# Eight pairs' statistics moved from VectorE to ScalarE, new idle products on TensorE, and new orders for all five engines

## The reference

```
layer 0 and 1 (graph attention):
    h = x W^T;  e_ij = leaky(h_i.a_src + h_j.a_dst, 0.2), -inf where adj == 0
    layer(x) = softmax_j(e) h
layer 2:
    e_ij = leaky(sum_d x_id a0_d x_jd, 0.2)     # adj == 1 takes e0; 2, 3, 4 don't occur in a 0/1 matrix
    layer(x) = (sigmoid(e) where adj == 1, else 0) x + bias2
layer 3:
    layer(x) = ((adj == 1) x) W3[0] + bias3
layernorm: (x - mean) / sqrt(var + 1e-5), over the 128 features
```

## Time and profile before

| | us |
|---|---|
| three runs, median (lowest, highest) | 241.93 (241.18, 242.17) |
| the profiled execution's own time | 242.28 |
| its span, from first to last instruction | 240.2 |
| busy: TensorE, its weight loads, VectorE | 221.1, 205.2, 217.6 |
| busy: ScalarE, GpSimd | 190.6, 171.6 |
| mean granted TensorE clock | 0.979 of full speed |

### The profile page before, as it was taken

The page is one execution under the profiler, slowest core; times in us unless marked ns, Lnnn a source line. Parts: engine busy times, 40 slices in busy tenths (PEclk is TensorE's granted clock), DMA queues, the critical chain, the costliest instruction groups (busy, mean ns, idle before and its releaser), DMA issues.

```text
span 240.2 us, 5686 instructions
## 1 busy us (share of the span) xinstructions
PE 221.1 (92%) x1737; PEld 205.2 (85%) x1737; DVE 217.6 (91%) x716; ACT 190.6 (79%) x613; POOL 171.6 (71%) x262
## 2 busy tenths in 40 slices
PE   7598998999999999999999999999999999799760
PEld 7497977898979999999989999999999899799650
DVE  1568997999999998999999999999999999999992
ACT  2466799696989788857877998698866999999872
POOL 5120541399889878866497988694989989999991
PEclk9979999999999999999999999999999999999995
DMA  7996910332322100801400580004000021000115
GB/s 178 257 199 152 239 50 5 129 50 42 44 90 46 66 26 0 264 1 44 134 1 4 87 262 3 1 4 132 3 0 0 3 89 48 0 0 3 45 42 183
DMA packets 12144, 17.56 MB, mean 73 GB/s; under 512 B 1104, under 2 KB 5968, under 8 KB 12112
## 3 DMA queue, kind: packets, MB, share of 16 engines
q1 hardware_dynamic: 9520, 12.85, 16.4%
q0 software_dynamic: 2304, 4.20, 10.7%
q10 hardware_dynamic: 288, 0.14, 0.2%
HBM read 17.17 MB, written 4.19 MB: 89 GB/s over the span
## 4 chain that ended last, share of the span: by engine, by line
PE 73%; DVE 14%; ACT 5%; issue 3%; DMA 3%; POOL 1%; DVEq 0%; POOLq 0%
PE banks L1189 32%; PE banks L1124 10%; PE banks L1156 10%; PE banks L1146 5%; PE banks L1109 4%; PE banks L1186 4%; PE banks L1166 4%; DVE fstats L918 3%; DMA mask_all<-adj_turned 3%; DVE wgt_all L865 3%; DVE fres_all L910 3%; DVE fres_all L898 2%; ACT odd_square L610 1%; PE banks L1134 1%; ACT wgt_all L665 1%
## 5 line engine op out<-in xcount | busy, mean ns | idle before, releaser
L547 POOL TENSOR_TENSOR frstd<-fvar,minus_half 128x4 f32<-128x4 f32 x64 | 65.1, 1023 | 15.6 <-DVE fvar L924 6.2
L1189 PE MATMUL banks<-vals_all,wgt_all 128*128 128x129 f32 x512 | 63.6, 279 | 0.0
L1189 PEld LDWEIGHTS banks<-vals_all,wgt_all 128*128 128x128 f32 x512 | 61.0, 194 | 1.0
L865 DVE SCALAR_TENSOR_TENSOR wgt_all<-banks,gain,mask_all 128x256 f32<-128x256 f32 x128 | 52.5, 470 | 0.8 <-DMA mask_all<-adj_turned 0.4
L918 DVE BATCH_NORM_STATS2 fstats<-fres_all 128x6 f32<-128x256 f32 x128 | 46.9, 414 | 0.1
L542 POOL TENSOR_TENSOR xb_all<-xs_all,bias_cen 128x256 f32<-128x256 f32 x64 | 45.3, 732 | 1.0 <-ACT xs_all L692 0.9
L692 ACT ACTIVATE xs_all<-fres_all,frstd 128x128 f32<-128x128 f32 x112 | 35.9, 404 | 1.4 <-POOL frstd L547 1.3
L1189 PE MATMUL banks<-xs_all,wgt_all 128*128 128x128 f32 x256 | 31.3, 276 | 1.5 <-DVE wgt_all L873 1.4
L1189 PEld LDWEIGHTS banks<-xs_all,wgt_all 128*128 128x128 f32 x256 | 29.9, 192 | 2.0 <-DVE wgt_all L873 1.9
L1156 PE MATMUL banks<-fxT,fxTa 128*128 128x256 f32 x128 | 30.3, 382 | 0.0
L1156 PEld LDWEIGHTS banks<-fxT,fxTa 128*128 128x128 f32 x128 | 23.1, 190 | 2.8 <-issue 0.2
(11 more groups left out here) (92 smaller groups left out, 400.7 us busy)
## 6 DMA issues: line engine op xcount, KB each, us to landing
xT_all<-x_turned SPq DMA_DIRECT2D x16, 256.0 KB, 3.2
mask_all<-adj_turned POOLq DMA_DIRECT2D x16, 256.0 KB, 4.7
x_all<-x_laid SPq DMA_DIRECT2D x16, 256.0 KB, 4.0
out<-xs_all SPq DMA_DIRECT2D x16, 256.0 KB, 2.3
bias<-biases_laid SPq DMA_DIRECT2D x1, 128.0 KB, 6.1
w_pack<-W_and_columns ACTq DMA_DIRECT2D x1, 68.0 KB, 3.1
w_fast<-W_turned ACTq DMA_DIRECT2D x1, 64.0 KB, 3.4
w_nat<-in_L_gnn_W SPq DMA_DIRECT2D x1, 64.0 KB, 6.2
```

Source lines behind the costliest of these rows:

```text
L547: nc.gpsimd.tensor_tensor(frstd[:, int(l), slot(n), :], fvar[:, int(l), slot(n), :], minus_half[:, :, :], ALU.pow).then_inc(fast_pool[k], 1)
L865: last = nc.vector.scalar_tensor_tensor(out=wgt(u)[:, c, :], in0=place(f"rows{l}", u), scalar=gain[:, u, c, 1:2], in1=maskT(u)[:, c, :], o ...
L1189: last = nc.tensor.matmul(place(f"out{l}", u)[:, b * width:(b + 1) * width], wgt(u)[:, c, b * P:(b + 1) * P], (vals if l in "01" else xs)( ...
```

## The change

1. ScalarE gets a step `stats` (function `statistics`). Eight pairs' statistics go there from VectorE: `stats2:6`, `stats2:9`, `stats3:1`, `3:3`, `3:4`, `3:6`, `3:7`, `3:8`. For each graph it runs two ACTIVATEs with the function Square over a 128x128 block, which write their squares into `xs` (overwritten later by the norm) and add up a row into `fstats` column 2. The two functions `variances` that looked for `stats` on VectorE now ask `doer`.
2. Idle products: a word `idle:87` puts 8 products into bank 7, without a wait; `idle:97` 9 into bank 7. `warm:3` and `warm:4` are gone, and `warm:5` is there in place of the latter.
3. The last pair's (`SHARED = 15`) final norm is split: VectorE normalizes its first graph and SyncE stores it; ScalarE's new step `last:15` normalizes the second graph and issues its store from its own queue.
4. All five lists and `BANKS` are written anew. Most steps move by a few places. These change engine: `logits0:5` from VectorE to ScalarE; `norm2:1` from VectorE to ScalarE; `norm1:0`, `1:3`, `1:7`, `1:12` from ScalarE to GpSimd and `norm1:5` back; `xTa:7`, `xTa:9` from ScalarE to GpSimd and `xTa:1` back; `bias2:3` and five `fscale` from GpSimd to VectorE, one `fscale` the other way; and some `var`.

Of the tables the diff shows two lines of ScalarE's and two of TensorE's.

```diff
--- before.py
+++ after.py
@@ -55,6 +55,7 @@
 H = 2
 TEAMS = 16
 AHEAD = 6
+SHARED = 15
 X_IN, XT_IN, MASK, XS, FXT, FXTA, VALS, WGT, SG, FRES, XB = 4, 3, 16, 6, 7, 5, 6, 7, 2, 9, 5
 
 
@@ -62,116 +63,115 @@
 ORDER = {
...
     "pe": (
-        "h0:1 h0:0 rows0:1 dT0:1 turn:0 top0:1 dT0:0 warm:3 rows0:0 top0:0 out0:1 warm:4 h0:3 h0:2 dT0:3 h0:4 top0:3 "
+        "h0:1 h0:0 dT0:1 rows0:1 dT0:0 idle:87 turn:0 top0:1 idle:97 top0:0 rows0:0 out0:1 warm:5 h0:3 h0:2 dT0:3 h0:4 "
...
     "act": (
-        "logits0:1 gains0:1 logits0:0 seen:1 v0:1 gains0:0 vals0:1 v0:0 seen:2 seen:3 vals0:0 logits0:2 logits0:3 "
+        "logits0:1 gains0:1 seen:1 logits0:0 v0:1 gains0:0 vals0:1 seen:3 v0:0 seen:2 vals0:0 logits0:2 logits0:3 "
...
-WHOLE = tuple(n + l for n in ("dT", "top", "gains", "v", "logits", "peak", "dmax", "rsum", "rinv", "var", "center", "pow") for l in "0123") + ("fscale", "seen", "res2", "res3")
+WHOLE = tuple(n + l for n in ("dT", "top", "gains", "v", "logits", "peak", "dmax", "rsum", "rinv", "var", "center", "pow") for l in "0123") + ("fscale", "last", "seen", "res2", "res3")
@@ -203,7 +203,7 @@
         if name in apart:
             continue
         for u in graphs(n):
-            if u == n * H or name + layer not in WHOLE:
+            if u == n * H or name + layer not in WHOLE and (name + layer, n) != ("norm3", SHARED):
                 value[n % K] += 1
             found[name + layer, u] = value[n % K]
     return found, value
@@ -212,7 +212,7 @@
 UP_SQUARE = UP * UP
 
 
-COUNTS = {"pe": counts("pe", apart=("turn", "warm")), "act": counts("act"), "dve": counts("dve", apart=("centre", "judge")), "pool": counts("pool", apart=("mask",))}
+COUNTS = {"pe": counts("pe", apart=("turn", "warm", "idle")), "act": counts("act"), "dve": counts("dve", apart=("centre", "judge")), "pool": counts("pool", apart=("mask",))}
 
 
 def at(engine, name, u):
@@ -483,6 +483,9 @@
             def store(l, n, k):
                 normer = doer("norm3", n)
                 sp.wait_ge(signals[normer][k], at(normer, "norm3", final(n)))
+                if n == SHARED:
+                    sp.dma_start(out[n * H], xs(n * H)[:, :, :]).then_inc(fast_stored[n % XS], 16)
+                    return
                 sp.dma_start(out[n * H:(n + 1) * H].rearrange("h p b d -> p h b d"), xs_all[:, pair(n, XS), :, :]).then_inc(fast_stored[n % XS], 16)
 
             def load_weights(l, n, k):
@@ -495,7 +498,7 @@
             sp.wait_ge(redo_set, 1)
             again = sp.value_load(redo_i[0:1, 0:1], min_val=0, max_val=1)
             for q in range(XS):
-                sp.wait_ge(fast_stored[q], 16 * len(range(q, TEAMS, XS)))
+                sp.wait_ge(fast_stored[q], 16 * (len(range(q, TEAMS, XS)) + (q == SHARED % XS)))
             with sp.If(again):
                 sp.dma_start(w3[:, 1:R, :], W3[1:R].rearrange("r d o -> d r o")).then_inc(gen_w3_in, 16)
                 for k, vector in enumerate((bias2, bias3)):
@@ -571,7 +574,8 @@
                     nc.gpsimd.tensor_scalar(fxTa(u)[:, :], fxT(u)[:, :], a2[:, 0:1], None, ALU.mult).then_inc(fast_pool[k], 1)
 
             def variances(l, n, k):
-                pool.wait_ge(fast_dve[k], at("dve", f"stats{l}", final(n)))
+                squarer = doer(f"stats{l}", n)
+                pool.wait_ge(signals[squarer][k], at(squarer, f"stats{l}", final(n)))
                 squares, var = fstats[:, slot(n), :, 2], fvar[:, int(l), slot(n), :]
                 factor, floor = VARIANCE[l]
                 nc.gpsimd.tensor_scalar(var, squares, factor, floor, ALU.mult, ALU.add).then_inc(fast_pool[k], 1)
@@ -692,13 +696,31 @@
                             last = nc.scalar.activation(xs(u)[:, b, :], fres(u)[:, b, :], ACT.Copy, scale=frstd[:, int(l), u, b:b + 1])
                     last.then_inc(fast_act[k], 1)
 
+            def statistics(l, n, k):
+                adder = doer(f"res{l}", n)
+                for u in graphs(n):
+                    act.wait_ge(signals[adder][k], at(adder, f"res{l}", u))
+                    for b in range(NB):
+                        last = nc.scalar.activation(xs(u)[:, b, :], fres(u)[:, b, :], ACT.Square, accum_out=fstats[:, u, b, 2:3])
+                    last.then_inc(fast_act[k], 1)
+
             def variances(l, n, k):
-                act.wait_ge(fast_dve[k], at("dve", f"stats{l}", final(n)))
+                squarer = doer(f"stats{l}", n)
+                act.wait_ge(signals[squarer][k], at(squarer, f"stats{l}", final(n)))
                 factor, floor = VARIANCE[l]
                 nc.scalar.activation(fvar[:, int(l), slot(n), :], fstats[:, slot(n), :, 2], ACT.Copy, bias=floor, scale=factor).then_inc(fast_act[k], 1)
 
-            steps = {"seen": note_odd, "var": variances, "xT": copy_xT, "logits": logits, "gains": gains, "v": exponentials, "vals": values, "xTa": copy_xTa, "sigmoid": sigmoids,
-                     "high": high_part, "agg": copy_gathered, "norm": normalize}
+            def last_norm(l, n, k):
+                u = final(n)
+                act.wait_ge(fast_pool[k], at("pool", "pow3", n * H))
+                for b in range(NB):
+                    normed = nc.scalar.activation(xs(u)[:, b, :], fres(u)[:, b, :], ACT.Copy, scale=frstd[:, 3, u, b:b + 1])
+                normed.then_inc(fast_act[k], 1)
+                act.wait_ge(fast_act[k], at("act", "last", n * H))
+                act.dma_start(out[u], xs(u)[:, :, :]).then_inc(fast_stored[n % XS], 16)
+
+            steps = {"stats": statistics, "seen": note_odd, "var": variances, "xT": copy_xT, "logits": logits, "gains": gains, "v": exponentials, "vals": values, "xTa": copy_xTa, "sigmoid": sigmoids,
+                     "high": high_part, "agg": copy_gathered, "norm": normalize, "last": last_norm}
             for step, l, n in order("act"):
                 steps[step](l, n, n % K)
 
@@ -812,7 +834,7 @@
                         dve.wait_ge(fast_stored[n % XS], 16 * (n // XS))
                 else:
                     dve.wait_ge(fast_pool[k], at("pool", f"pow{l}", n * H))
-                for u in graphs(n):
+                for u in graphs(n)[:1 if (l, n) == ("3", SHARED) else H]:
                     for b in range(NB):
                         if l == "1":
                             last = nc.vector.tensor_scalar(xs(u)[:, b, :], fres(u)[:, b, :], frstd[:, 1, u, b:b + 1], fcenter[:, u, b:b + 1], ALU.mult, ALU.add)
@@ -918,7 +940,8 @@
                     nc.vector.bn_stats(fstats[:, u, :, :].rearrange("p b k -> p (b k)"), fres(u)[:, :, :].rearrange("p b d -> p d b")).then_inc(fast_dve[k], 1)
 
             def variances(l, n, k):
-                dve.wait_ge(fast_dve[k], at("dve", f"stats{l}", final(n)))
+                squarer = doer(f"stats{l}", n)
+                dve.wait_ge(signals[squarer][k], at(squarer, f"stats{l}", final(n)))
                 squares, var = fstats[:, slot(n), :, 2], fvar[:, int(l), slot(n), :]
                 if l == "1":
                     nc.vector.scalar_tensor_tensor(out=var, in0=squares, scalar=1 / D, in1=fvar[:, 0, slot(n), :],
@@ -1207,7 +1230,9 @@
             pe.wait_ge(ident_bf_set, 2)
             sequence = order("pe")
             for q, (step, l, n) in enumerate(sequence):
-                if step == "warm":
+                if step == "idle":
+                    idle_products(n // 10, n % 10)
+                elif step == "warm":
                     following, layer, m = sequence[q + 1]
                     keep_warm(n, following + layer, m * H)
                 else:
```

## The result

The changed kernel takes 246.10 us (median of 4 runs, 244.69 to 247.26), the kernel before 241.79 us in the same comparison (241.18 to 242.17). The ratio is 1.018, with a 95% interval from 1.015 to 1.022: 4.3 us slower. The prediction was 244.4 us, slower, with a range of 240.4 to 246.4. The direction holds, and so does the first half of the term called deciding, a TensorE held by the mask. The fall of the clock behind it, its other half, did not come, and two of the smaller terms have the wrong sign. That the total still lies in the range is in part luck.

The account below looks back on a forecast made before the run. TensorE's pace was taken to bound the middle, its handoffs with VectorE the start and end. 242.28 + 3.4 - 0.5 - 0.2 - 0.2 = 244.8 us, less 0.35 for the profiled execution: 244.4 us, range 240.4 to 246.4.

Parts of the forecast that it names:

- the term called deciding: Start of the lists: TensorE held about 3 us by the mask, then a clock fall; 3.4 us late.
- The fall of the clock: Start, behind the wait: clock at half speed for 4 us, adding 2.0 us; likelier 2 to 1.
- the prediction's case of a wait without the fall: Start: h0:2 ends at 20.4 us, 1.7 us late, clock staying up; kernel 242.7 us, chance 0.22.
- The rival in which the idle products work as they read: Start: logits0:0 before 8 us, no TensorE gap, clock at 1.00; kernel 239.3 us, chance 0.13.
- The middle (-0.5 us): From 60 to 200 us: VectorE's relief meets a full TensorE and wins only 0.5 us.
- net about 5 us off: VectorE's busy time: 5.9 us of statistics and norm2:1 leave, bias2:3, fscale and var come; net about 5 us less.
- The Trainium skill's rule that it weighed: Middle: judge TensorE by the weight loads' busy share; several microseconds could be won; the prediction's counting decided against it.
- ScalarE (10 to 16 us, taken 13): ScalarE's added busy time for 32 squares, 0.32 to 0.51 us each depending on whether the read hides.
- the 124 named as a sign: From 60 to 200 us: ScalarE busy for 124 us or more, beside a full TensorE.
- The rival in which ScalarE is late: Middle: vals and xT copies wait behind squares, TensorE waits 2.4 us more; kernel 246.8 us, chance 0.08.
- The end (-0.4 us): End: 0.2 us won by the shared last norm and store, 0.2 us by earlier res3:10 and out3:12.

Follow-up runs that it names:

- Kernel four: The kernel before with the changed start alone (mask wait ahead of logits0:0 and dT0:0, plus the new idle products); 244.96 us, ratio 1.012.
- kernel five: The changed kernel with the last pair whole again: last:15 removed, one norm on VectorE, one store; 246.14 us, ratio 1.018.
- Kernel seven: The changed kernel with the eight pairs' statistics back on VectorE, all other orders as changed; 248.19 us, ratio 1.028.
- kernel one: The changed kernel with one swap on ScalarE: logits0:0 ahead of seen:1 again; 245.16 us, ratio 1.014.
- kernel three: The kernel before with the new idle products alone, nothing newly waiting for the mask; 242.60 us, ratio 1.003.
- kernel ten: The kernel before with the eight pairs' statistics as squares on ScalarE, and var2:9 on GpSimd; 253.40 us, ratio 1.049.
- kernels five and six: Five has its own line. Six: the kernel before with only the last pair's norm shared and its store split; 241.74 us, ratio 1.003.

## Why the prediction held, and where it did not

**The start (+3.4 us): the wait held, the fall of the clock did not come in the changed kernel.** Kernel four shows the whole mechanism alone: 3.3 us, a wait of 2.98 us (3 was said), `logits0:0` at 10.47 (10.3 to 10.5), the fall of the clock, `h0:2` near 22.2 (22). But some 1.1 us of the 3.3 are a longer end, so the start itself is about 2.2 us, between the prediction's 1.7 without a fall and its 3.4, and its three runs without a fall have only 1.1 us.

What the profile after shows is the prediction's case of a wait without the fall, with an earlier mask: `logits0:0` at 8.96, a wait of 1.42. With a mask about as late as in the earlier trace rows kernels five and seven have `h0:2` ending at 20.60 and 20.38 us, where this case said 20.4. The sized part that failed is the fall, 2.0 us of the 3.4, taken as likelier by 2 to 1. Kernel four ran the same instructions behind its wait and had the fall in three of six runs, so why the changed kernel stayed free of it isn't shown. In this changed kernel's four runs the mean clock is 0.987 to 0.990, in kernel four's it is below 0.984 in three of six. The other error is to have taken the landing of the mask from one execution: over the traces `seen:1` starts between 7.8 and 9.5 us, with the DMAs ahead of it in nearly the same order. The prediction said that nothing brings the mask earlier, and priced one draw.

The rival in which the idle products work as they read was priced at 239.3 us. Its start was seen once, in the trace of kernel one: `logits0:0` before 8 us, no gap, the clock at 1.00, `h0:2` ending at 17.32, as the rival says. As a price for the kernel it fails: kernel three has the products and no held `logits0:0`, and its twelve runs took 240.6 to 244.2 us. The runs of the kernel before speak against the price too. Seven of them with a mean clock of 0.979 or 0.980 took 241.3 to 242.1 us, beside medians of 241.6, and five with 0.974 to 0.981 took 243.2 to 244.1: the 2 us at half speed in the earlier trace rows are not 2 us of the kernel's time in every execution.

**The middle (-0.5 us) failed in sign.** It is 0.7 to 1.5 us longer in four traces. The step that failed is "net about 5 us off" VectorE: in the middle it is 0.2. `bias2:3` was priced at 0.8 us and took 1.9, the `var` steps at 1.0 and took 2.4. Of the 2.4 us only 0.8 are the six `var` that came to one group. The other 1.6 are the fourteen that were there, whose mean rose from 215 to 327 ns, and 1.1 of the 1.9 of `bias2:3` are the same thing: in the new order they meet GpSimd's products of two tiles and end only with them. The prediction priced instructions by what they take alone, by which `bias2:3` would be 0.82 us, and had no term for this overlap; in all VectorE loses 2.9 us more by it than before. That it is the overlap follows from the ends, which lie 0.02 us apart in every case of `var`; no run took it away. Kernel seven adds what the middle is worth to VectorE: 4.7 us of busy time more, 3.4 us of middle. So once the middle has grown, VectorE binds it as much as TensorE does, and the prediction's reading, that it goes at TensorE's pace, was too one-sided. The Trainium skill's rule that it weighed (Perfetto Trace Analysis, "Identifying the Most-Contended Engine") would have let the middle win several microseconds. No kernel won any there. But none of them relieved VectorE without a new wait, so that the rule isn't refuted by these runs. An unchanged load explains why nothing was won, and not why 0.7 to 1.5 us were lost. That the new orders make these is argued, and not shown.

**ScalarE (10 to 16 us, taken 13) is nearer 9.** The squares and their reads, by instruction, in the changed kernel:

```profile
L704 ACT ACTIVATE xs_all<-fres_all x32: 293/321/373, 88.5 to 184.6; 128x128 f32<-128x128 f32 x32
L704 ACT ACTIVATION_READ_ACCUMULATOR xs_all<-fres_all x32: 187/212/253, 88.7 to 184.8; 128x1 f32 x32
```

The read hides part of itself: in kernel ten a square starts 0.29 us after the one ahead of it with the read in between. 32 of them are 9.3 us. ScalarE's busy time in the middle differs by 8.8 us between kernel seven and the changed one. From 60 to 200 us ScalarE has 120.95 us, not the 124 named as a sign. The rival in which ScalarE is late did not come in the change (in its middle TensorE never waits over 0.6 us for ScalarE), and did in kernel ten, at 10 us and not 2.4.

**The end (-0.4 us) failed in sign: +1.5 us in the profile.** The prediction followed data to the last store and stopped there. The norm and the store it priced well (no difference by the medians, kernels five and six). What it lacked is the way from there to the barrier, which it held to be the same.

**The sum.** By the runs: start 2.2, middle and VectorE's late drain 1.3 to 1.7, TensorE's late drain 0.5 to 1.1, the shared pair 0 to 0.6. These are 4.0 to 5.6 us for 4.3 measured. The start is that of kernel four, half of whose runs had the fall, so it is the least certain of them; the trace of kernel five gives 1.7, 1.4 and 1.2 us for start, middle and end. The prediction had 2.5 us, with 2.0 for a fall that didn't come in it and 0.9 taken off for a middle and an end that in fact lost some 2.5. These errors have opposite signs and partly cancel, so that its range held by some luck. No kernel tried is faster than the one before.

## What to carry to other kernels

A wait that an in-order engine meets early is harmless until something is queued behind it that another engine's order puts first. When two lists are changed together, look for such a pair before pricing either edit: here the prediction found it in the two lists and in one row of the trace. An instruction that may have to wait for a transfer, or for a step of another engine, goes behind everything others need soon: `seen:1`, `stats3:7` and `fscale:13` each held TensorE for 1.4 to 3.7 us from engines with idle time to spare. And when a load is taken off a full engine, count what the same change puts back on it, and look at what the neighbouring engine runs at the same time: 5.4 us of VectorE's busy time in the changed kernel are instructions drawn out under a product on GpSimd.

## What was not expected of the hardware

- A VectorE instruction over 4 columns with two inputs took 0.15 us alone and up to 0.73 when it met a GpSimd product of two 128x256 tiles, and then ended 0.02 us behind it (eight cases in the changed kernel, three before). Matches with GpSimd's power or its norms show no such delay (0.14 to 0.16 us).
- VectorE's last step came 3.9 to 4.5 us after the last product in all traces, and still the end varied from 7.6 to 9.4 us, by when VectorE and TensorE reached the barrier. After the stores the DMA queues carry only a few fetches of instructions there (0.04 MB in 3 us). VectorE's delay goes by its count of instructions, in steps, and sixteen memsets at its start moved it by 1.4 us, nine by 1.8. That the fetches cause the delay is argued from their place, not shown.
- The granted clock fell in some executions of the same kernel and not in others: 0.979 to 0.992 over the span in six runs of kernel four.
- The landing of one input moved by 1.7 us between executions of kernels that issue it nearly alike (7.8 to 9.5 us), nearly as much as the start lost.
